# A graph network's gather: SyncE's single rows issued one group earlier in its own order of work

## What is computed

```
h = node_features @ enc_W + enc_b
for l in range(3):
    cat = concatenate([h[src], h[dst], edge_features], -1)      # 64 + 64 + 16
    m = relu(cat @ msg_W1[l] + msg_b1[l]) @ msg_W2[l] + msg_b2[l]
    agg = segment_sum(m, dst)
    h = gru_cell(agg, h, gru_Wih[l], gru_Whh[l], gru_bih[l], gru_bhh[l])
out = layernorm(x + relu(h @ ro_W1 + ro_b1) @ ro_W2 + ro_b2)
```

## Time and profile before

| | us |
|---|---|
| median of 3 runs (6051.36 to 6051.94) | 6051.45 |
| the profiled execution's own time | 6053.24 |
| its span, first to last instruction | 6051.5 |
| POOL busy | 4492.2 (74%) |
| DVE busy | 3922.5 (65%) |
| PE busy | 3017.8 (50%) |

### The profile page before, as it was taken

How to read it: one execution, slowest core, us unless ns; L and a number is a source line. 1 busy time by engine, 2 the same in 40 slices (tenths; PEclk the granted TensorE clock), 3 DMA queues, 4 the chain that set the end, 5 groups by cost and what they waited for, 6 DMA issues and landing times.

```text
span 6051.5 us, 74086 instructions
## 1 busy us (share of the span) xinstructions
PE 3017.8 (50%) x8058; PEld 1662.4 (27%) x8058; DVE 3922.5 (65%) x5593; ACT 418.0 (7%) x612; POOL 4492.2 (74%) x4701
## 2 busy tenths in 40 slices
PE   5555555555555454444444444445444444444444
PEld 4232232222322232222222222223222222222222
DVE  5788888887787656555555555556665555555565
ACT  1000000000000000000000000000000000000001
POOL 7777777777777747777777777777777777777776
PEclk7666666666666666666666556666666666666665
DMA  5334333333332312222222222222222222222221
GB/s 148 72 69 87 77 76 79 73 82 74 69 84 59 64 36 53 48 48 50 45 48 48 48 48 48 48 44 50 49 49 48 49 45 48 48 48 48 48 48 34
DMA packets 566789, 353.40 MB, mean 58 GB/s; under 512 B 315065, under 2 KB 454417, under 8 KB 565808
## 3 DMA queue, kind: packets, MB, share of 16 engines
q0 software_dynamic: 150080, 154.46, 14.3%
q1 hardware_dynamic: 271659, 142.98, 9.1%
q10 hardware_dynamic: 144528, 51.15, 3.6%
HBM read 307.51 MB, written 40.49 MB: 58 GB/s over the span
## 4 chain that ended last, share of the span: by engine, by line
POOL 47%; issue 21%; SPq 14%; DVE 9%; ACTq 4%; PE 3%; DMA 2%; ACT 0%; DVEq 0%; POOLq 0%
POOL p_src L1074 47%; SPq L649 10%; SPq L645 3%; DVE work_ps L1973 2%; ACTq L649 2%; DVE pool_sb L1888 1%; DMA p_src<-p_tab 1%; DVE p_src L1970 1%; DVE folds L2008 1%; ACTq L645 1%; PE bank L1300 0%; SPq L882 0%; PE work_ps L1225 0%; PE bank L1301 0%; PE bank L1222 0%
## 5 line engine op out<-in xcount | busy, mean ns | idle before, releaser
L1074 POOL DMA_INDIRECT p_src<-p_tab,idx_all x4603 | 4398.5, 956 | 1451.3 <-issue 1407.3
L1970 DVE TENSOR_TENSOR p_src<-work_ps,p_src 128x512 f32<-128x512 f32 x602 | 414.4, 688 | 1731.3 <-DMA p_src<-p_tab,idx_all 1422.5
L1244 PE MATMUL bank<-hot,folds 128*128 128x96 f32 x2408 | 625.5, 407 | 1611.2 <-DVE folds L2008 1584.7
L1225 PE MATMUL work_ps<-w_edges,msg 128*128 128x512 f32 x1204 | 1055.8, 976 | 24.5 <-DMA windows_sb<-q_tab 24.5
L1244 PEld LDWEIGHTS bank<-hot,folds 128*128 128x128 f32 x2408 | 503.2, 290 | 1886.0 <-DVE folds L2008 1803.8
L2003 DVE SCALAR_TENSOR_TENSOR work_ps<-work_ps,rel 128x1024 f32<-128x1024 f32 x602 | 741.8, 1232 | 20.8
L1973 DVE TENSOR_TENSOR work_ps<-p_src,bank 128x1024 f32<-128x1024 f32 x602 | 739.7, 1229 | 20.6
L2008 DVE TENSOR_REDUCE folds<-work_ps 128x256 f32<-128x1024 f32 x602 | 732.6, 1217 | 5.8
L1238 PE MATMUL bank<-hot,enc_w 128*16 128x96 f32 x832 | 154.7, 333 | 846.7 <-DVE folds L2008 843.8
L1300 PE MATMUL bank<-state,gate_w 128*128 128x468 f32 x324 | 258.5, 896 | 438.5 <-DVE chunk_sum L2028 334.3
L1238 PEld LDWEIGHTS bank<-hot,enc_w 128*16 128x16 f32 x832 | 81.0, 120 | 965.7 <-DVE folds L2008 937.1
(11 more groups left out here) (233 smaller groups left out, 2273.2 us busy)
## 6 DMA issues: line engine op xcount, KB each, us to landing
p_src<-p_tab ACTq DMA_DIRECT2D x9408, 0.2 KB
p_src<-p_tab SPq DMA_DIRECT2D x9408, 0.2 KB
p_src<-p_tab,idx_all POOLq DMA_INDIRECT x4666, 3.6
msg<-pack_edges SPq DMA_DIRECT2D x98, 256.0 KB
pick<-pack_rel_tab SPq DMA_DIRECT2D x196, 96.0 KB
pool_sb<-in_pack_attrs SPq DMA_DIRECT2D x56, 288.0 KB, 3.2
pack_edges<-dst_i ACTq DMA_DIRECT2D x224, 64.0 KB
msg<-in_edge_k SPq DMA_DIRECT2D x52, 256.0 KB
```

Of the source, the lines that this page charges most:

```text
L1074: pool.indirect_dma_start(out=p_src[r][0:rows, t, :], out_offset=None, in_=p_tab[l][0:NODES, :], in_offset=bass.IndirectOffsetOnAxis(ap=id ...
L1225: nc.tensor.matmul(edge_ps[k % 2], attrs[n % 2][:, s, :], w1_edges[:, l, :], start=True, stop=True)
L1244: last = nc.tensor.matmul(fold_ps, folds[:, b, :], hot_all[n % 2][:, s * BLOCKS + b, 1:WINDOW + 1], start=(b == 0), stop=(b == BLOCKS - 1))
L1970: nc.vector.tensor_tensor(rows, edge_ps[k % 2], rows, ALU.add).then_inc(with_edge, 1)
```

## The change

SP's single rows move by one iteration: iteration `g` now issues those of group `g - 1`, not of group `g - 2`, ahead of the loads of group `g`. The first group's come in front of the loop, and the call behind layer 0's loop is gone. The number of DMAs is the same. ACT, POOL, PE and DVE run the same instructions in the same order.

```diff
                     if l == LAYERS - 1:
                         fast_rows(0)
+                    single_rows(sp, mybir.EngineType.SP, l, GROUP - 1, 0, SP_ROWS, sp_singles)
                     for g in range(2, GROUPS_OF[l]):
-                        single_rows(sp, mybir.EngineType.SP, l, GROUP * (g - 2) + GROUP - 1, 0, SP_ROWS, sp_singles)
+                        if g - 1 < SINGLES_OF[l]:
+                            single_rows(sp, mybir.EngineType.SP, l, GROUP * (g - 1) + GROUP - 1, 0, SP_ROWS, sp_singles)
                         if l == 0:
                             batch, at = job(g - 1)
...
                             shift_counts(g // 2 - 1)
                             chunk_nodes(g // 2 + 1)
                     if l == 0:
-                        single_rows(sp, mybir.EngineType.SP, l, STEPS - 1 - GROUP, 0, SP_ROWS, sp_singles)
                         shift_counts(LOOPED - 1)
                         shift_counts(LOOPED)
```

## The result

| | before | after |
|---|---|---|
| median of 4 runs each, us | 6051.69 (6051.36 to 6052.75) | 5975.48 (5971.02 to 5977.99) |
| profiled execution, us | 6053.24 | 5977.99 |
| its span, us | 6051.5 | 5976.2 |

The ratio is 0.9872, with an interval of 0.9858 to 0.9886: 76.2 us less, where 80.3 us were forecast. The two profiled executions differ by 75.25 us. Lines behind the changed loop stand one number higher after (1074 is 1075, 1970 is 1971); those ahead of line 938 keep theirs.

A forecast was written before the change was run, and what follows sets the result against it. A loop through SP, not POOL, was taken to pace layer 0. POOL's slot waits (35.8 us) plus DVE's end lag (44.5 us) make 80.3 us, so 6051.45 us becomes 5971.1 us; range 5962 to 6016 us.

The forecast's parts named there:

- The pacing loop: Layer 0: SP's shift waits for DVE, DVE for SP's rows; a pair took 81.8 us against POOL's 78.3 us.
- Layers 1 and 2 give nothing: Layers 1 and 2: POOL bounds them, so earlier single rows gain nothing there.
- Term A: Layer 0, 180 to 1860 us: POOL's waits for slots that DVE frees go, 35.8 us.
- Term B: End of layer 0: DVE's lag behind POOL's last gather shrinks from 54.1 to 9.6 us, a gain of 44.5 us.
- The sum: Whole kernel: slot waits and end lag of layer 0 together save 80.3 us, giving 5971.1 us.
- The start: Start of layer 0: late loads and planes cost DVE 5 to 15 us, the span nothing, at most 6 us.
- SP's wait at the shift: Layer 0, line 889: SP's wait there, 8.5 us each before, would stay above 5 us.
- The cost of `joined`: SP's new wait order: nothing after a shift, nearly over in layer 0's other groups, some microseconds per group in layers 1 and 2.
- Rival 3: Layer 0: loads come late and SP becomes the bound; 9.5 us more per pair is some 15 us slower; chance 0.10.
- Rival 1: Layer 0: ACT's rows take SP's place as the limit, giving 5990 to 6025 us; chance 0.18.
- Rival 2: Layer 0: POOL's gathers slow as DVE gets denser, some 11 us lost, 5982 us; chance 0.05.
- Signs: Layer 0: some 79 gathers per 100 us, DVE waiting on POOL's tiles; POOL's pause between layers under 10 us.

The follow-up runs named there:

- Parts 3: 50 of POOL's gathers in layer 0 left out: on the kernel before 6051.77 us, on the changed kernel 5949.45 us.
- part 6: Kernel before, rows unmoved, in layer 0 ACT issues the shift and SP's node load goes behind the rows: 5977.84 us; same move on the changed kernel: 5971.82 us.
- part 1: The change put into the kernel before in layer 0 only: 5979.91 us; in layers 1 and 2 only: 6049.13 us.
- part 2: The change put into the kernel before for layer 0's groups from 43 on only: 6042.51 us; for its groups 0 to 42 only: 5983.60 us.
- part 5: Changed kernel with the old order of rows for groups 0 to 3 of layer 0: 5976.43 us.
- part 7: Changed kernel with four, then ten more address loads per layer 0 group, absent from the programs that ran: 5977.30 us and 5978.10 us.
- part 4: Changed kernel with ACT's pieces of single rows issued one step earlier (AHEAD_OF 6 for 5): 5974.77 us.

## Why the prediction came out right, and where it did not

- **The pacing loop: right.** SP waits at the shift for DVE, DVE for SP's rows. Parts 3 and 6 show it from both sides: less POOL work gives nothing, and cutting the loop elsewhere gives the same time. The pair that the prediction read took 81.8 us; over steps 23 to 175 a pair took DVE 80.3 us.
- **Layers 1 and 2 give nothing: right** (part 1).
- **Term A, 35.8 us: nearly right.** By the same count, 7.4 - 13 x 0.30 = 3.5 us of slot waits are left, so 32.3 us went.
- **Term B, 44.5 us: right in size, wrong in how.** The lag fell from 54.1 to 9.3 us, 44.8 us. But the step "0.8 us in each of 42 groups, and then some 9 us in each of the last seven" fails: part 2 shows that DVE can't make up 9 us in a group, since SP needs 67 us or more for a pair and the shift comes late. It was made up earlier. The lag was 52.4 us at step 23, 45.0 at step 55 and 11.5 at step 175: (52.4 - 11.5)/38 groups = 1.1 us each, instead of 0.8. A DVE pair took 76.3 us over these steps, by which it is nearly as slow as POOL's 78.3 us. The size came out right because it was capped by "as short as it can", and that the cap was reached is in part luck: the last seven groups could not do what was asked of them, and the 42 before did more than was asked.
- **The sum, 80.3 us, is 4 us too large** by the medians and 5 by the profiled executions. A and B gave 32.3 + 44.8 = 77.1 us. POOL's first gather of layer 0's step 4 is 3.7 us later than before (92.14 for 88.47 us), which no term had; that leaves 73.4 us against 74.3 seen at step 207. Most of the 3.7 us is not the change's: the end of step 4's gathers lies between 97.0 and 99.8 us in the profiled executions of the kernels that start as the one before, and between 97.5 and 101.9 us where they start as the changed one.
- **The start: 5 to 15 us of DVE were 17.8.** 3.1 of them are there at step 4 already. The late loads cost 4.2 us in step 6, as forecast (some 5), and DVE waits for no planes. The rest is the first shift, which stood behind one more set of rows: DVE waited 16.0 us for it, through PE, and 3.3 us before. The prediction had looked at loads and planes only. That it costs no span was right (part 5).
- **SP's wait at the shift "stays above 5 us": wrong.** 32.0 us over the 20 shifts that waited 173.6 us before is 1.6 us each. The cost of `joined` was put at nothing or a few microseconds. The wait there took 67 us more in 1600 us, and part of the reserve went there. In all SP still waits 200.0 us, some 10 us for each pair of groups, but no longer mainly at the shift, so the shift itself comes late at times. Rival 3's sign was to be seen there, at PE's wait for `shifted`, not at lines 1862 or 1888. No run shows that it cost time, and none shows how much more work SP could take (part 7). The rival's own price was off in one place: by its figures 9.5 us more per pair are (71.3 + 9.5 - 80.0) x 25 = 20 us, not 15.
- **Rival 1, ACT in SP's place: no.** ACT's rows are the last ones now (37.4 us of waits), but with them early the time is the same (part 4).
- **Rival 2, POOL slows: no.** DVE's busy share in 180:1860 rose from 81.1% to 84.4% (1363.2 and 1418.1 of 1680 us), and the gather took 957 ns both times. The lock that the Trainium skill describes (SBUF — State Buffer, "SBUF: two separate sides") may be there, but nothing of it shows with this mix of instructions: layer 0's gathers are 3 to 4 ns longer than layer 1's after as before.
- **Signs.** 1329 gathers in 1680 us are 79.1 in each 100 us, as said, and the pause between the layers is gone. DVE waiting for POOL's tiles in layer 0 came only from step 181 on.

## What to carry to other kernels

An engine that works through its code in order can make a loop out of a wait: look for the instruction it stands at longest, ask what urgent work is queued behind it, and whether the releaser waits for that work. Such a loop can pace a stage while the busiest engine looks nearly saturated; a trial that leaves out some of the busiest engine's work tells the two apart. And when urgent work is moved ahead, look at everything it is now ahead of: here the shift, not the loads, became the late one.

## What was not expected of the hardware

- The mean time of an indirect gather moves a little from one execution to the next, in every stage alike. In the profiled execution of the kernel in part 6 (5989.65 us, where its other runs took 5973.9 to 5978.9) 4603 gathers took 960 ns each, for 955 in the changed kernel, and 958 for 953 ns in layer 1, where nothing had been changed. Part 7's first kernel, which has the changed kernel's instructions, shows what it is worth. Its profiled execution took 5989.43 us, 11.4 us more than the changed kernel's. Its gathers were busy 4413.4 us for 4396.0 us, 17.4 us more; POOL came to the end of step 4 3.8 us earlier, and its slot waits were 2.6 us shorter. 17.4 - 3.8 - 2.6 = 11.0 us is nearly all of the difference. Why the gather's time moves stays open.
- Issuing a row of 256 bytes from SP cost the same 0.39 us, with its share of the address loads, in all rows shown here: 64 took 24.92 to 25.30 us, also in part 2, where SP issued without a stop for 67 us.
